# Column rows in the score stage, byte addresses in the step tables, and fewer rests of GpSimd in a chain of graph layers

## The reference

```python
# L0, three times: weighted mean over incoming edges
agg = segment_sum(e_w[:, None] * h[src], dst) / clip(segment_sum(e_w, dst), 1)
h = layernorm(relu(agg @ Wn.T + h @ Wr.T + b)) * g + b2
# L1: edge network
ef  = (relu(edge_attr @ We1 + be1) @ We2 + be2) * sigmoid(t @ Wt + bt)
out = x + segment_sum(relu([x[row], ef] @ Wn1 + bn1) @ Wn2 + bn2, col)
# L2, twice: 8 relations
h = segment_sum((x @ W[r])[src, etype8], dst) + x @ Wl + b
# L3, twice: graph transformer with 32 edge types, 8 heads of 16
a   = sum_over_head(kT[src, etype32] * q[dst])          # score of an edge
att = softmax of a over the edges of one dst
hag = segment_sum(vT[src, etype32] * att, dst)
```

## Time and profile before

| | us |
|---|---|
| three runs, median (lowest to highest) | 6493.9 (6492.3 to 6510.6) |
| the profiled execution, its own time | 6516.9 |
| its span in the profile | 6515.1 |
| PE busy | 3454.9 (53%) |
| DVE busy | 2199.7 (34%) |
| ACT busy | 1126.3 (17%) |
| POOL busy | 3210.2 (49%) |
| mean granted TensorE clock | 0.658 of full |

### The profile page before, as it was taken

How to read it: one execution, slowest core, us unless ns; L and a number is a source line. 1 busy time by engine, 2 the same in 40 slices (tenths; PEclk the granted TensorE clock), 3 DMA queues, 4 the chain that set the end, 5 groups by cost and what they waited for, 6 DMA issues and landing times. The chain is left out here.

```text
span 6515.1 us, 60996 instructions
## 1 busy us (share of the span) xinstructions
PE 3454.9 (53%) x14685; PEld 2426.0 (37%) x14685; DVE 2199.7 (34%) x5075; ACT 1126.3 (17%) x2416; POOL 3210.2 (49%) x3406
## 2 busy tenths in 40 slices
PE   5555777767774555633453336644435266444353
PEld 3333545445552333332333322244335222333353
DVE  3222222322224223311121114433348444333485
ACT  0000222222222111100000002310105233011053
POOL 4665566556654665466556651066540410655403
PEclk7666777676676666655665557755558677555586
DMA  2111334333432332311131128944434489444343
GB/s 60 47 47 37 92 100 100 88 90 96 100 94 83 91 91 67 109 47 47 59 115 47 46 61 335 395 129 130 127 97 141 122 347 386 127 128 127 96 140 99
DMA packets 600939, 772.17 MB, mean 119 GB/s; under 512 B 89734, under 2 KB 507000, under 8 KB 588064
## 3 DMA queue, kind: packets, MB, share of 16 engines
q1 hardware_dynamic: 480000, 492.16, 22.6%
q0 software_dynamic: 120608, 276.12, 16.2%
HBM read 416.10 MB, written 351.82 MB: 118 GB/s over the span
## 5 line engine op out<-in xcount | busy, mean ns | idle before, releaser
L453 POOL DMA_INDIRECT arena<-table,idx_s x3128 | 2989.8, 956 | 2458.4 <-issue 995.9
L735 PE MATMUL ps<-arena,work 128*128 x4160 | 968.1, 370 | 953.0 <-issue 884.8
L735 PEld LDWEIGHTS ps<-arena,work 128*128 128x128 f32 x4160 | 815.3, 269 | 1207.8 <-issue 1207.4
L1917 PE MATMUL ps<-ident,onehot 128*128 128x128 f32 x832 | 217.7, 413 | 671.5 <-DVE onehot L429 543.5
L433 DVE TENSOR_SCALAR work<-iota_row,dl_s,w_s 128x128 f32<-128x128 f32 x1248 | 351.6, 361 | 456.7 <-issue 316.1
L429 DVE TENSOR_TENSOR work<-ps,dl_s 128x512 f32<-128x512 f32 x208 | 143.9, 692 | 934.1 <-issue 612.4
L1877 DVE TENSOR_TENSOR arena<-arena,ps 128x128 f32<-128x128 f32 x832 | 183.9, 283 | 806.5 <-POOLq L449 382.5
L1917 PEld LDWEIGHTS ps<-ident,onehot 128*128 128x128 f32 x832 | 142.2, 207 | 728.8 <-DVE onehot L429 588.4
L909 DVE SCALAR_TENSOR_TENSOR arena<-ps,vecs,arena 128x256 f32<-128x256 f32 x208 | 100.7, 484 | 896.2 <-ACT arena L888 440.9
L1928 PE MATMUL ps<-arena 128*128 x1664 | 391.4, 413 | 5.1 <-issue 3.6
L1928 PEld LDWEIGHTS ps<-arena 128*128 128x128 f32 x1664 | 352.7, 313 | 26.5 <-issue 17.1
(11 more groups left out here) (329 smaller groups left out, 4139.0 us busy)
## 6 DMA issues: line engine op xcount, KB each, us to landing
table<-arena SPq DMA_DIRECT2D x96, 2048.0 KB
values<-arena SPq DMA_DIRECT2D x832, 64.0 KB
arena<-values SPq DMA_DIRECT2D x208, 256.0 KB
arena<-table,idx_s POOLq DMA_INDIRECT x3128
arena<-edge_times SPq DMA_DIRECT2D x208, 128.0 KB
edge_part<-arena SPq DMA_DIRECT2D x208, 128.0 KB
table<-arena SPq DMA_DIRECT2D x50, 512.0 KB
arena<-edge_part SPq DMA_DIRECT2D x98, 256.0 KB
```

The costliest lines, as they stand in the source:

```text
L453: pool.indirect_dma_start(ring[:, ds(t % RING * 2 * H, width)], None, tab, bass.IndirectOffsetOnAxis(ap=idx_s[:, t:t + 1], axis=0)).then_i ...
L735: mm = pe.matmul(accf[:, ds(b, P)], o, ring[:, ds(slot, H)], start=False, stop=False, skip_group_check=True)
L1917: mm = pe.transpose(ps[:, q % 2, c * P:(c + 1) * P], onehot[:, 4 * q + c, :], ident[:, :])
```

## The change

1. **Column rows in the score stage.** During the table phase of the first L3 layer, TensorE turns the table of local targets `dl_s` once and it is stored as `col_rows` in DRAM, one row of 512 numbers for each quad. In the score pass ScalarE's queue loads row n to all 128 partitions, and VectorE compares it with the partition's own number: that gives the turned one-hot at once, up to 7 quads ahead, in a ring of 12. The transposes and ScalarE's copies go; the query products use all 8 PSUM banks.
2. **Byte addresses.** `blk_i` and `slot_i` hold byte addresses in PSUM and SBUF. Registers are taken afresh for each load and released behind the last use. The edge passes load two quads at a time.
3. **Rests.** `rest` goes from 4 to 6 in the first aggregation and the joining pass, 2 to 3 in the edge passes, 4 to 8 in the relation passes, 2 to 8 in the score passes.

```diff
+        def addresses(eng, source, base, first, top):
+            regs = [eng.alloc_register(f"at_{next(loads)}") for c in range(source.shape[1])]
+            eng.load(regs, source)
+            return regs, [eng.snap(r, donate=True, min_val=base + 4 * first, max_val=base + 4 * top, guaranteed_mod_val=0, out_of_modulus=4) - base
+                          for r in regs]
...
-                ch(dve.tensor_scalar(turn_f, turn_f, float(2 * H), None, ALU.mult))
+                ch(dve.tensor_scalar(turn_f, turn_f, float(8 * H), float(ring_at), ALU.mult, ALU.add))
...
         def step_blocks(pe, j, n=U):
-            pe.load(first_cols[0:n], blk_i[0:1, ds(j, n)])
-            return [pe.snap(r, min_val=0, max_val=(NB - 1) * P) for r in first_cols[0:n]]
+            regs, places = addresses(pe, blk_i[0:1, j:j + n], PSUM_AT, 0, (NB - 1) * P)
+            return regs, [v // 4 for v in places]
...
-                    gathers(pool, tab, H, freed, rest=2 if edges else 4)
+                    gathers(pool, tab, H, freed, rest=3 if edges else 6 if sums else 8)
...
-                    gathers(pool, table, H, freed, joins, rest=4)
+                    gathers(pool, table, H, freed, joins, rest=6)
...  (key_value_table_phase, first layer only)
+                            for c in range(4):
+                                mm = pe.transpose(ps[0:ALL_QUADS, 7, c * P:(c + 1) * P], dl_s[:, c::4], ident[:, :])
+                            act.activation(turned_cols, ps[0:ALL_QUADS, 7, :], ACT.Copy).then_inc(cols_copied.sem, 1)
+                            sp.dma_start(col_rows, turned_cols).then_inc(cols_stored.sem, 16)
+                            if columns and n == 1:
+                                pe.wait_ge(cols_copied.sem, cols_copied.at(1))
...  (score_phase)
-                        gathers(pool, table32, 2 * H, freed, rest=2)
+                        gathers(pool, table32, 2 * H, freed, rest=8)
...
+                    @block.scalar
+                        for n in range(ALL_QUADS):
+                            if n >= QUADS:
+                                act.wait_ge(onehot_ready.sem, onehot_ready.at(n - QUADS + 1))
+                            act.dma_start(cols_ring[:, n % QUADS, :], col_rows[n, :].partition_broadcast(P)).then_inc(row_in[n % QUADS].sem, 16)
...
+                        def across(n):
+                            dve.wait_ge(row_in[n % QUADS].sem, row_in[n % QUADS].at(16 * (n // QUADS + 1)))
+                            if n >= DEEP:
+                                dve.wait_ge(made.sem, made.at(n - DEEP + 1))
+                            dve.tensor_scalar(across_ring[:, n % DEEP, :], cols_ring[:, n % QUADS, :], node_no[:, 0:1], None,
+                                              ALU.is_equal).then_inc(onehot_ready.sem, 1)
...
+                        for n in range(AHEAD):
+                            across(n)
+                        for n in range(ALL_QUADS):
+                            if n + AHEAD < ALL_QUADS:
+                                across(n + AHEAD)
+                            multiply(n)
+                            if n > 0:
+                                reduce(n - 1)
...
-                                mm = pe.transpose(ps[:, q % 2, c * P:(c + 1) * P], onehot[:, 4 * q + c, :], ident[:, :])
-                                act.activation(onehotT[:, q % 2, :], ps[:, q % 2, :], ACT.Copy).then_inc(evac.sem, 1)
-                                mm = pe.matmul(ps[:, 4 + q, c * P:(c + 1) * P], onehotT[:, q % 2, c * P:(c + 1) * P],
+                                mm = pe.matmul(ps[:, n % 8, c * P:(c + 1) * P], across_ring[:, n % DEEP, c * P:(c + 1) * P],
                                                Qn_flat[:, ds(b, P)], start=True, stop=True)
```

186 lines of the change are left out of this document (98 added, 88 removed).

## The result

The changed kernel was no faster: 6545.2 us median (6525.3 to 6563.6, five runs) beside 6494.3 us for the kernel before in the same comparison, ratio 1.0066 (95% interval 1.0046 to 1.0086). The forecast was 6192 us, ratio 0.953, and its range ended at 6265. Every ratio compares fast executions only; one of 7130 us, of six of a kernel on chip 0 (old rests outside the score pass), is left out.

What follows compares the result with a forecast made beforehand. GpSimd's gather issue was taken to bound all eight passes. Rests 338 us, less 12 row loads, 10 compare, 12 TensorE's pace and 2 setup, gave 302 saved: 6494 to 6192 us, range 6120 to 6265.

Steps and rivals of the forecast that it cites:

- GpSimd's issue sets the length of all eight passes; all other engines follow it: All eight gather passes: 489 us of gathers each, the rest of 552 to 615 us mostly rests.
- what is late next when a rest is gone: nothing at GpSimd: Quad hand-overs: gathers have landed one quad behind, so removed rests leave no new GpSimd wait; no loss counted.
- rival 1: TensorE paces the light passes; with the second edge pass 58 us lost instead of 12, 6238 us; chance 0.15.
- Three in a row pass at 0.30 us: Light passes: three boundaries without a rest in a row cost GpSimd only 0.30 us, as evidence that gathers land in time.
- Rests, 338 us: All eight passes: fewer GpSimd waits for landed gathers, each worth 2.0 to 2.6 us, save 338 us.
- Row loads, 0.5 us a rest, 12 us: Score passes: new broadcasts slow landings by 0.5 us at each of 12 rests left, 12 us lost for both.
- New compare, 5 us a pass: Score passes: VectorE's compare from SBUF stretches some gathers, 5 us a pass, 10 in all; upper end 38 a pass.
- rival 2: Score passes: the port VectorE and GpSimd share costs 38 us a pass instead of 5, 6258 us; chance 0.10.
- rival 5: Score stage: row loads, gathers and stores jam the DMA engines; 6670 us at double price; chance 0.03.
- Byte addresses, 0 where GpSimd bounds: TensorE, VectorE and SyncE queues: saved address work stands beside GpSimd, so worth 0 where GpSimd bounds.
- TensorE's pace, 12 us: Light passes and second edge pass: TensorE's crawl costs 12 us, between a gain of 30 and a loss of 58.
- The forecast is wrong if gaps over 1 us appear at hand-overs without a rest: GpSimd's quad boundaries in the new profile: sign against the forecast, which expected the plain 0.30 us there.

Runs made afterwards that it cites:

- rests alone: Only the five new rest numbers, against the kernel before: ratio 0.9449 on chip 0, 0.9461 on chip 4, 1.0250 on chip 11.
- fixed places: Byte addresses and new rests, old score pass, but TensorE loads no registers in the fifth pass: 283 us of slow issue there, 319 in the sixth.
- pauses: Byte-address kernel, old score pass; last four passes have 3, 1, 6, 3 waited fills per quad instead of rests: passes 602, 551, 693, 598 us.
- even pausing: Byte-address kernel, old score pass, rests 6, 2, 2, 4, then two waited fills per quad in the last four passes: 6473.7 us, ratio 0.9877 to before.

## Why the prediction was wrong

The failed step is the first one, on which the sum stands: "GpSimd's issue sets the length of all eight passes; all other engines follow it", and with it "what is late next when a rest is gone: nothing at GpSimd". It holds on chips 0 and 4. On the chip of the forecast's own profile, and on 9 and 11, a second bound lay just beneath: TensorE in the passes 1, 5 and 6, VectorE in 4, the hand-overs between TensorE, ScalarE and VectorE in the edge passes, SyncE in the score passes, all of them slowed beside GpSimd's issue. A rest costs GpSimd about 2 us and gives the others that time at full speed. Without it they slow down more, so the bound beneath rises to meet the saving. It is rival 1's mechanism, for which the forecast had 58 us in the light passes and the second edge pass. Over all eight passes it takes the whole 338 us: counted from gather to gather, the edge and joining passes lose 50 us, the first pass 2, and only the relation and score passes keep something, 9 and 33 us.

The evidence lay in the trace of before. TensorE's group in the sixth pass shows 305 us of "issue" against 15 us of waiting for VectorE, an engine that can't keep up, in a pass that the forecast called GpSimd's. I looked for idle time on GpSimd and took TensorE's crawl for an exception that most stretches recover from. "Three in a row pass at 0.30 us" is true of most but not, as the forecast says, of all boundaries without a rest: in the trace of before 9 of them stand over 1 us, 2, 4 and 3 in the passes 1, 5 and 6, 31 us in all. One of them, from the sixth pass:

```profile
3515.01 0.94 POOL L453 DMA_INDIRECT arena<-table,idx_s  x1 [3.90 <-remote]
```

The others prove only that the ring of 60 slots had not filled yet. That the rests kept it from filling is my reading; in the changed kernel the first such wait comes at the fifteenth quad, when the ring is full, in passes 1, 5, 6, 7 and 8.

Step by step:

- **Rests, 338 us.** Right where the engines issue normally: 353 us on chip 0. A rest was worth 2.3 us in the first pass (540.7 - 522.4 over 8; put at 2.0), 2.2 in the relation passes (2.0), 2.0 in the joining pass (2.1), 2.4 in the edge passes (38 over 16; 2.3) and 2.6 in the score passes (612.4 - 518.7 over 36; 2.5 and 2.6).
- **Nothing is late next.** Wrong in the first comparison and on chips 9, 11 and 14, see above.
- **Row loads, 0.5 us a rest, 12 us.** As put on chip 4: a rest of the changed kernel's score passes stands for 3.26 and 3.24 us beside 2.75 and 2.65 in rests alone, 0.5 and 0.6 more, 13 us in all. On chip 0 it was 0.8 with 12 rests a pass and 0.9 with 48, where it came to 43 us a pass. The column rows pay for themselves only by the other terms, of which none was seen: on chip 4 the changed kernel stands 0.5% above rests alone.
- **New compare, 5 us a pass.** 2 to 3 us: gathers of 951 and 952 ns instead of 945. The shared port (rival 2) took nothing like its 38 us. The rule of the Trainium skill ("SBUF — State Buffer", "SBUF: two separate sides") that was weighed there is not refuted by this, since a compare mostly begins inside a gather: 85 and 77 of the 104 did on chip 4. But where a gather began while a compare ran, 22 and 31 times, it took over 1 us only 7 and 10 times, so the trace does not show the rule at its fullest either.
- **DMA share 0.73.** 0.72 on chip 4; rival 5 (a jam) did not come.
- **Byte addresses, 0 where GpSimd bounds.** Right on chip 0 (1.0001). With slow issue and the new rests they give some 30 us a score pass, which the forecast did not see.
- **TensorE's pace, 12 us.** It failed in size as well as in place: the first pass, the second edge pass and the two relation passes were to save 16 + 37 + 24 + 24 = 101 us by their rests and got 11 us longer from gather to gather, 112 us lost where 12 were put and 58 in rival 1.
- "The forecast is wrong if gaps over 1 us appear at hand-overs without a rest": they did. 45 and 43 boundaries of the edge passes have them where 32 rests stand, 20 and 25 of the score passes where 12 stand. As a sign it was weak, since 9 such gaps stood in the trace of before.

What stays open: what couples the other engines' issue to GpSimd's, and why chips 0 and 4 are free of it. It is not TensorE's register work (fixed places) and not the landing of the gathers (pauses). The profile shows no instruction fetch that would explain it. TensorE's 29856 instructions match packets of 16 KB (q8, 1.90 MB over 116 packets, 257 instructions each). In the first pass there are 8 such packets, on chip 4 too, and the median packet of the kernel takes 0.99 us there and 0.96 on chip 4. Packets of 16 KB are what the Trainium skill ("Runtime: NRT & Kernel Launch", section "Instruction fetch mechanics") also describes, and that page expects their cost to be mostly hidden.

```profile
q8 instruction: 116, 1.90, 0.1%
```

The row is that of the changed kernel, the same on every chip. Whether slow issue belongs to the chip for good is not shown either: chip 11 had it in both sets, though before took 6558 us in one and 6503 in the other, every other chip ran in one set only, and no chip was seen in both kinds; the number of the first comparison's chip is not recorded. The edge passes' late hand-overs were not tried by themselves; that they go away on chips 0 and 4 together with slow issue speaks for one cause, but was not tested. Nor was even pausing run on a chip without slow issue, where I expect rests alone (0.945) to remain the best.

## What to carry to other kernels

A wait that looks like pure loss on the bounding engine may be what keeps the others at speed. Before removing it, read what the consumers' idle time is made of: "waiting for the producer" leaves room, "issue" for half of a pass means that they are the next bound, however free their busy share looks. Slow issue that is gone is not yet time won, though: the pass with a rest at every quad took 697 us and the one with none 556. And price such a change on more than one chip: the same kernel gave 0.945 and 1.025.

## What the runs showed of the hardware

- In the first comparison and on chips 9, 11 and 14, TensorE, VectorE and SyncE issue instructions 0.7, 1.4 or 2.1 us apart in stretches of 3 to 80 us (0.70 us steps in the timeline of the first pass) while GpSimd issues one indirect gather every 1.25 us; on chips 0 and 4 never. The kernel before took 6494 to 6558 us there and 6402 to 6430 here.
- A pause of 1.1 us in GpSimd's issue every 6 us stops it (0 us in the fifth pass), one of 0.76 us nearly so (13 and 0 us in the relation, 75 and 79 us in the score passes), one of 0.25 us does not (351 us), and 1.1 us every 11 us leaves most of it (202 and 225 us). Full-speed issue of the other engines came back without GpSimd waiting for its last gathers to land.
- 104 broadcasts of 2 KB to 128 partitions beside the gathers and stores make a wait for the landing of a gather 0.9 us longer on chip 0 with 48 such waits a pass (DMA share 0.58), 0.8 us with 12 (0.71), and 0.5 to 0.6 us on chip 4 with 12 (0.71).
